# A graph network on one core: dense pass and GIN 1 in one block, weights and segments in one phase, scans in GIN 2 and GCN

## What is computed

```python
def _gin_conv(x, src, dst, wa, ba, wb, bb):
    agg = jax.ops.segment_sum(x[src], dst, num_segments=N_NODES)
    h = x + agg
    h = jnp.maximum(h @ wa + ba, 0.0)
    return h @ wb + bb
# L0: two GIN convolutions 128->64->64 and 64->256->256, then @ wl + bl
# L1 (RGCN): msg = x[src] * edge_norm; sum per (relation, dst); 4 bases mixed by w_comp
# L2 (GCN): y = x @ W.T; out = segment_sum(deg^-1/2[row] * deg^-1/2[col] * y[row], col) + bias
# L3 (GAT): 3 layers of attention with edge attributes, each with its own layer norm
x = _layernorm(x + L0(x)); x = _layernorm(x + L1(x)); x = _layernorm(x + L2(x)); x = _layernorm(x + L3(x))
```

## Time and profile before

| | us |
|---|---|
| median of 3 runs | 3941.27 (3938.68 to 3960.31) |
| the profiled execution, its own time | 3940.17 |
| its span, first to last instruction | 3938.4 |

### The profile page before, as it was taken

One profiled execution on the slowest core, in us unless ns is written; L12 is line 12 of the kernel. 1 busy time (PEld: TensorE's weight loads), 2 busy tenths in 40 slices (PEclk: granted clock), 3 DMA queues, 4 the chain that ended last, 5 costly groups with the idle time before them and its releaser, 6 DMA issues. The chain is left out here.

```text
span 3938.4 us, 83380 instructions
## 1 busy us (share of the span) xinstructions
PE 2910.5 (74%) x19323; PEld 2360.3 (60%) x19323; DVE 2669.5 (68%) x9708; ACT 2397.4 (61%) x6301; POOL 2318.7 (59%) x2526
## 2 busy tenths in 40 slices
PE   3999997815886999688588799177991778884662
PEld 2777776603443666344366699177991767883562
DVE  3999998804333566799688744387443978887873
ACT  2999987701322566466456566186771877874873
POOL 3777777776761774677578577301772027721766
PEclk7999999957997999899799999588995998876755
DMA  2667779613442444355456599265992669973541
GB/s 79 213 217 239 261 262 176 139 30 97 128 128 70 116 133 120 120 158 159 128 171 192 180 300 299 72 190 180 302 296 63 198 209 285 282 247 105 146 144 52
DMA packets 427200, 678.04 MB, mean 172 GB/s; under 512 B 81253, under 2 KB 161726, under 8 KB 427064
## 3 DMA queue, kind: packets, MB, share of 16 engines
q1 hardware_dynamic: 352664, 554.64, 44.5%
q0 software_dynamic: 74400, 121.87, 12.7%
HBM read 384.98 MB, written 295.47 MB: 173 GB/s over the span
## 5 line engine op out<-in xcount | busy, mean ns | idle before, releaser
L540 POOL DMA_INDIRECT msgs<-t_gat,row_i x600 | 577.9, 963 | 681.9 <-POOLq L123 484.9
L1636 PEld LDWEIGHTS n_p_q<-mean_col,n_sq 128*128 128x128 f32 x2352 | 309.7, 205 | 0.0
L1636 PE MATMUL n_p_q<-mean_col,n_sq 128*128 128x1 f32 x2352 | 299.4, 248 | 0.0
L2245 POOL DMA_INDIRECT out_rows<-a_res,a_stage x200 | 201.8, 1009 | 124.1 <-issue 84.5
L2263 PE MATMUL a_p_t<-ident,a_wm 128*128 128x128 f32 x600 | 120.6, 334 | 199.9 <-DVE a_wm L2344 199.8
L532 POOL DMA_INDIRECT g_ring<-t_h,g_g_stage x200 | 199.6, 998 | 77.4 <-issue 48.5
L540 POOL DMA_INDIRECT msgs<-in_x,src_i x200 | 205.6, 1028 | 64.3 <-issue 64.3
L567 POOL DMA_INDIRECT t_where<-slot_id,own_i x200 | 202.6, 1013 | 67.1 <-issue 67.1
L1475 PE MATMUL rg_p_b<-bases,rg_gt 128*128 128x512 f32 x400 | 207.0, 622 | 43.7 <-DVE rg_mg L1581 41.6
L582 POOL DMA_INDIRECT row_i<-t_where,src_i x200 | 200.8, 1004 | 64.4 <-issue 63.6
L1957 ACT ACTIVATE n_nt<-n_p_t,cxt 128x512 f32<-128x512 f32 x294 | 200.2, 681 | 61.4 <-PE n_p_t L1931 61.1
(11 more groups left out here) (391 smaller groups left out, 9335.9 us busy)
## 6 DMA issues: line engine op xcount, KB each, us to landing
n_h<-t_gat SPq DMA_DIRECT2D x294, 264.0 KB
t_gat<-n_hn SPq DMA_DIRECT2D x196, 264.0 KB
t_x<-de_x SPq DMA_DIRECT2D x196, 256.0 KB
a_h<-t_gat SPq DMA_DIRECT2D x150, 264.0 KB
t_gat<-a_hn SPq DMA_DIRECT2D x100, 264.0 KB
t_gat<-de_h SPq DMA_DIRECT2D x98, 264.0 KB
g_xd<-t_xd SPq DMA_DIRECT2D x100, 256.0 KB
n_x<-t_x SPq DMA_DIRECT2D x98, 256.0 KB
```

The lines of the kernel that those rows point to most:

```text
L540: self.nc.gpsimd.indirect_dma_start(out=self.msgs[:, c, 0:width], out_offset=None, in_=table, in_offset=bass.IndirectOffsetOnAxis(ap=idx[: ...
L1636: last = self.nc.tensor.matmul(p_q[:, j:j + 1], sq[:, j * D:(j + 1) * D], self.mean_col[:], start=True, stop=True)
L2245: nc.gpsimd.indirect_dma_start(out=self.out, out_offset=bass.IndirectOffsetOnAxis(ap=stage[:, u, j:j + 1], axis=0), in_=res[:, u, j, :], i ...
```

## The change

Six things are changed together.

1. **One start phase.** `phase_start` puts both first phases in one block. Segment loads stay on Sync, the 26 weight loads go to Scalar's queue; POOL clears, then builds the weights' constants, then tells the segment constants; Vector runs `find`, then `fold`; TensorE the two turns. `fold` also centres `bases`, `wg` and `bg` (their means over the output features are taken off).
2. **One block for the dense pass and GIN 1.** POOL runs `slot_gathers` and then at once `map_gathers`; a barrier between the two parts joins the four other engines only. Memory of the two parts is shared through `part`. TensorE waits for the message gathers and Sync for the stores of `t_xd` explicitly. `row_i` is cleared to `SLOTS + N`, a row of zeros that Sync writes into `t_h1`.
3. **GIN 1 on Vector**: the sum L1147 now stands before the scan of the same step. Added is a sum of own rows and bias `bc` that goes back to `t_xd`, 256 KB a step, so that GIN 2 needs no bias. The hidden rows are kept in `msgs` (`hidden`).
4. **GIN 2 by the scan**: four transposes of the gathered rows to two PSUM banks, a scan, a sum with `hidden`, the two layers, `p_o` with two banks. One-hot matrices, carries, the load of the own rows and the bias sum are gone; a load of the flags is added. A ring buffer is freed by its transposes.
5. **RGCN**: since inputs and weights are centred, the layer norm is a square on Scalar, a reduce on Vector, a root, a reciprocal and a scale, one step later in the pipeline; `z` and the stores too.
6. **GCN by the scan**: transposes, scan, product with `wg` into two banks, then `v` = `dis` times product plus (x2 + bg) on Vector; norm as in RGCN; the copies of the GAT rows go to Scalar.

The core of the diff:

```diff
-        net.phase_weights()
-        net.phase_segments()
-        net.phase_dense()
-        net.phase_gin1()
+        net.phase_start()
+        net.phase_dense_gin1()
...
+    def phase_start(self):
...
+            @block.sync
+            def _(sp):
+                g_load(sp)
+                w_store(sp)
+                g_store(sp, zeroes)
+            @block.scalar
+            def _(act):
+                w_load(act)
+            @block.gpsimd
+            def _(pool):
+                g_clear, g_tell = g_fill
+                g_clear(pool)
+                w_fill(pool)
+                g_tell(pool)
+            @block.vector
+            def _(dve):
+                g_find(dve)
+                w_fold(dve)
...
+    def phase_dense_gin1(self):
+        nc = self.nc
+        ctx, sb, ps, sem = self.scope("dg")
+        with ctx:
+            ring = sb("g_ring", [128, UN, G4, D])
+            block = ctx.enter_context(nc.Block())
+            self.dense_part(block, lambda n: sem("de_" + n), ring, sem)
+            nc.multi_engine_barrier([e.engine for e in (nc.sync, nc.tensor, nc.scalar, nc.vector)])
+            self.gin1_part(block, lambda n: sem("g1_" + n))
...
             def _(pool):
                 nc.gpsimd.memset(x[:].rearrange("p a b c -> p (a b c)"), 0.0).then_inc(s["cleared"], 1)
-                self.slot_gathers(pool, sb, sem)
+                self.slot_gathers(pool, ring, pool_sem)
+                self.map_gathers(pool, pool_sem)
```

GIN 1 on Vector, one step:

```diff
+                    if live(k, u, 2, AG):
+                        dve.wait_ge(s["pe_x"], i - 1)
+                        dve.wait_ge(s["dve_s"], i - 1)
+                        wait(dve, s["pe_a"], i - 3)
+                        nc.vector.tensor_tensor(rt[:, u % 2], p_x[:], at[:, u % 2], ALU.add).then_inc(s["dve_r"], 1)
                     if live(k, u, 1, AG):
...
                         nc.vector.tensor_tensor_scan(at[:, w], fl[:, v], p_t[:, w], first, ALU.mult, ALU.add).then_inc(s["dve_s"], 1)
                     if live(k, u, 2, AG):
-                        dve.wait_ge(s["pe_x"], i - 1)
-                        dve.wait_ge(s["dve_s"], i - 1)
-                        wait(dve, s["pe_a"], i - 3)
-                        nc.vector.tensor_tensor(rt[:, u % 2], p_x[:], at[:, u % 2], ALU.add).then_inc(s["dve_r"], 1)
+                        dve.wait_ge(arrived[(u - 2) % UN], 16 * (k + (0 if u < 2 else 1)))
+                        self.stored(dve, outb, k, u, 2)
+                        nc.vector.tensor_tensor(xb[:, u % 2], xd[:, (u - 2) % UN], self.each(self.bc[:]), ALU.add).then_inc(s["dve_b"], 1)
```

GIN 2 on Vector, and GCN on Vector:

```diff
+                        nc.vector.tensor_tensor_scan(at[:, w], fl[0:H, f], p_t[0:H, w], start, ALU.mult, ALU.add).then_inc(s["dve_s"], 1)
...
+                        nc.vector.tensor_tensor(rt[:, u % 2], self.hidden(i - 2), at[:, u % 2], ALU.add).then_inc(s["dve_r"], 1)
...
+                        nc.vector.tensor_tensor(x2[:, w], x2[:, w], self.each(self.bg[:]), ALU.add).then_inc(s["dve_b"], 1)
...
+                            last = nc.vector.scalar_tensor_tensor(out=v[:, w, j, :], in0=p_g[:, w % 2, j * D:(j + 1) * D],
+                                                                  scalar=self.dis[:, bass.ds((i - 3) * G4 + j, 1)],
+                                                                  in1=x2[:, w, j, :], op0=ALU.mult, op1=ALU.add)
...
+                        nc.vector.tensor_reduce(ss[:, w], sq[:, u % 2], AXX, ALU.add).then_inc(s["dve_ss"], 1)
```

More of the change, by code:

```diff
@@ L211, in nodes, with weights_parts @@
         return v[bass.ds(UN * k + u - lag, 1), :, :, :].rearrange("g p j f -> p (g j) f")
-    def phase_weights(self):
+    def weights_parts(self, sb, ps, sem):
         nc, a = self.nc, self.a
-        ctx, sb, ps, sem = self.scope("wt")
-        with ctx:
[L218 to L251, removed]
@@ new lines, in load, with store, fill @@
+        def load(act):
+            with nc.allow_non_contiguous_dma(reason="columns of biases, once"):
+                for dst, src in loads:
+                    act.dma_start(dst, src).then_inc(loaded, 16)
+        def store(sp):
+            sp.wait_ge(zeroed, 1)
+            sp.dma_start(self.t4[SLOTS:SLOTS + 128, :], spread[:, 3, :]).then_inc(stored, 16)
+            sp.wait_ge(loaded, 16 * len(loads))
+            sp.wait_ge(stored, 16)
+        def fill(pool):
+            nc.gpsimd.memset(self.ident[:], 0.0).then_inc(ready, 1)
+            nc.gpsimd.memset(ones[:], 1.0).then_inc(ready, 1)
+            nc.gpsimd.memset(self.eps[:], EPS).then_inc(ready, 1)
+            nc.gpsimd.memset(spread[:, 3, :], 0.0).then_inc(zeroed, 1)
+            nc.gpsimd.memset(begin[:], 0.0).then_inc(self.begun, 1)
+            pool.wait_ge(ready, 3)
+            nc.gpsimd.affine_select(out=self.ident[:], in_=self.ident[:], compare_op=ALU.not_equal,
+                                    fill=1.0, base=0, pattern=[[-1, 128]],
+                                    channel_multiplier=1).then_inc(ready, 1)
+            nc.gpsimd.iota(self.iota[:], pattern=[[1, 128]], base=0, channel_multiplier=0,
+                           allow_small_or_imprecise_dtypes=True).then_inc(ready, 1)
@@ L550, in slot_gathers @@
         lag = 2
+        self.msgs_got = got
+        self.rows_stored = [(stored[u], 16 * ((AG - u + UN - 1) // UN)) for u in range(UN)]
         self.resident_gather(self.src_i, a["x"], D, got, bounds_check=N - 1, oob_is_err=False)
@@ L1797, in step @@
                         nc.scalar.activation(x3t[:], p_x[:], ACT.Copy).then_inc(s["act_x"], 1)
-                    carry(4)
-                    norm((2, 3))
-                steps(act, AG, 7, step, 3)
+                    if live(k, u, 6, AG):
+                        w = (u - 6) % UN
+                        act.wait_ge(s["dve_rs"], i - 5)
+                        self.stored(act, outx, k, u, 6)
+                        wait(act, s["pe_x"], i - 6 - UN + 1)
+                        for j in range(G4):
+                            last = nc.scalar.activation(x3[:, w, j, :], v[:, w, j, :], ACT.Copy, scale=rs[:, w, j:j + 1])
+                        last.then_inc(s["act_x3"], 1)
```

933 lines of the change are left out of this document (458 added, 475 removed).

## The result

The changed kernel takes 3776.4 us (median of 4 runs, 3771.0 to 3783.8); the kernel before took 3940.0 in the same measurement. The ratio is 0.958, with a 95% interval of 0.955 to 0.961. The prediction was 3774. The profiled execution took 3777.6 us, 2.1 of it outside the span (1.8 of 3940.2 before), so stage lengths of the two traces can be set side by side.

What follows compares the result with a forecast made beforehand. No front-half stage was taken as arithmetic-bound throughout; POOL's indirect DMAs set a floor in each. Start -19, dense pass and GIN 1 -82, GIN 2 -46, RGCN -4, GCN -15 sum to -166 from 3940.2: 3774 us, range 3750 to 3825.

Steps and rivals of the forecast that it cites:

- Start: Start phase: both sets of loads in flight together, segments worked first, then weights; 43 us and 1 for the border, -19 us.
- nearly half: Start phase before the change: nearly half of its 63.1 us said to be waiting for loads that could have overlapped.
- Dense pass and GIN 1: The merged block: POOL's unbroken program ends it, with the other engines' GIN 1 hidden 57 us ahead; -82 us (-79 to -85).
- 8.5 of landing and 1 of border: Gap of 9.55 us after POOL's last scatter, read as scatters landing (8.5) and about 1 for the phase border.
- The reorder itself is worth next to nothing here: GIN 1: with the old order's 6.16 us a step the end would be S + 1101, still ahead of POOL.
- GIN 1's own terms: GIN 1 beside POOL: head 22 us, 5.2 us a step for 49 steps, tail 30 us.
- GIN 2: GIN 2 by the scan: POOL bounds it at 5.2 us a step, drain 24 us; 285 for 331, -46 us (-30 to -54).
- RGCN: RGCN: POOL keeps gathers, stage copy and z, 5.09 + 1.04 + 0.3 = 6.43 against 6.52 us; -4 us (-12 to +8).
- GCN: GCN by the scan: POOL stays the bound, 5.2 us a step, drain 26 for 33; -15 us taken (0 to -22).
- (a): Rival: POOL misses its floor; GIN 2 at 5.5 us a step (-31), GCN unchanged; 3804 us, chance 13%.
- (b): Rival: GIN 1 not hidden, scatter and added store stretch its loads to 7.2 us a step; 3815 us, chance 10%.
- (d): Rival: TensorE's clock falls in GIN 1 and 2; 4079 us, passing no change at some two thirds low-level steps; chance 2%.

Runs made afterwards that it cites:

- held runs: Changed kernel with four engines waiting for the scatters at GIN 1's head: 3834.7 us with old GIN 2 and GCN; 3877.3 with old start, sum order and RGCN.
- The table: Dense pass and GIN 1 in the changed kernel: beside the scatters 1114.2 us (old sum order 1111.0, 1111.1); held behind them 1117.8 (old order 1183.7).
- the run with PSUM operands: Changed kernel with one operand of each step's two-SBUF Vector addition moved to PSUM in GIN 2 and GCN: 3759.1 us.
- the hold: Changed kernel with Sync, TensorE, Scalar and Vector waiting at GIN 1's head for the scatters' semaphore: 5632.7 us on the chip where the kernel before took 5740.
- the early gathers: Changed kernel with POOL's first 12 message gathers issued in the start phase: 5618.1 us on the slow chip; with PSUM operands in three stages, 3737.7 on an ordinary one.

## Why the prediction was right, and where it wasn't

**Start**, -19 forecast, -20.7 measured: right by its own steps (segments from 13.55 instead of 15). The two waits for loads are 33.5 of the 63.1 us, so over half of the old phase and not "nearly half".

**Dense pass and GIN 1**, -82 forecast, -78.7 measured: the mechanism was right, POOL's sum almost to the microsecond (829.5 forecast from the stage's start to the last scatter's end, 829.3 measured; map gathers 265 and 268). Two terms were wrong and offset each other in part. The 9.55 us of the earlier trace rows were read as 8.5 of landing and 1 of border. The held runs show a landing of 1.27 us, so what filled that gap was the pause of about 8.3 at the end of a phase. In the merged block that pause didn't vanish but moved to its end, 8.4 us, for which I had a border within 4; and the landing grew to 4.5 beside GIN 1's transfers, still 4 under the 8.5 put down for it, while the map gathers took 3 more. In sum 3 over the forecast, the upper end of its bounds.

**"The reorder itself is worth next to nothing here"** was right as it stood, 0 measured. But I credited the unbroken POOL with all of the 82. The table shows that letting GIN 1 begin beside the scatters is worth 4 us with the new order and 73 with the old one. The sum was never additive, since each edit removes the excess of the same longer chain over POOL's. GIN 1's own terms were right: head 20.6 (22), step 5.16 (5.2), tail 29.8 (30).

**GIN 2**, -46 forecast, -36.5 measured (-30 to -38 in the other traces, and 0 with GIN 2 of before put back). The pace was right (the last gather issued 262.8 us after the stage's start, 261 forecast); the drain was mis-sized, 31.3 us for the 24 I took "for a shorter chain". The row of GCN, 33, that I had beside it was the nearer one.

**RGCN**, -4 forecast, -16 measured in this trace, -8 to -13 in the six others that keep its new norm. Here a step of the sum failed: 5.09 + 1.04 + 0.3 put 0.3 of issue beside the product, and the traces show four gathers, copy and product in 6.12, the product right behind the last gather. With the statistics put back 1 step of 40 is at 6.12; without them 17 to 33. POOL's rounds of 6.52 in the earlier trace rows were not its floor. How the statistics on Vector hold POOL's rounds up was not tried.

**GCN**, -15 forecast, -6 measured (-7 to -11 in the others): groups of 5.25 (5.2 forecast), but a drain of 37.6 us, last gather issued at 2057.9 to 2095.5, where I took 26 for 33. The step that failed is the shortening: the pipeline has as many steps as before, and no ordinary trace of the new GCN drains in less than 33.8 (33.1 and 36.3 in the two of the old one). One thing that lengthens it is seen: TensorE was granted 0.69 of its full clock in this drain and 0.99 in the one before, and the last group's eight matmuls take 2.13 us instead of 1.17 (timelines of TensorE before and after). Over the eight traces of the new GCN the drain (33.8 to 37.6) doesn't follow the clock (0.69 to 0.84) trace by trace, so the clock's share stays open. Both drains erred in the same direction.

```profile
2248.06 1.17 PE L1629 MATMUL gc_p_h<-wx,gc_x3t 128*128 128x132 f32 x8 [0.69 <-ACT gc_x3t L1797]
...
2089.48 2.13 PE L1682 MATMUL gc_p_h<-wx,gc_x3t 128*128 128x132 f32 x8 [0.69 <-ACT gc_x3t L1812]
```

**Vector sums beside POOL.** By the run with PSUM operands, a Vector sum of two SBUF operands held POOL's gathers and copies back by 9.5 us in GIN 2 and 8.7 in GCN, of this trace's stages (8 to 16 and 4 to 9 against the six traces). The page "SBUF — State Buffer" of the Trainium skill, section "Who interferes with whom", says that a Vector instruction with at most one SBUF input, outside its two-port modes, doesn't contend with GpSimd, and that one with two does when GpSimd reads SBUF; the traces agree, 0 of 83 and 57 of 66 stretched.

**Rivals.** (a) came nearer than its 13% said: groups at 5.27 and 5.25, not at the floor, and -42 for GIN 2 and GCN together, between its -31 and my -61. (b) didn't come: GIN 1's loads stood the scatters, 5.16 a step. (d) didn't come: GIN 2 was granted 0.93 as before. But the clock did fall in GCN, from 0.95 to 0.79 of full speed. There TensorE has room in the groups, as (d) says, but not in the drain. Redone with its own terms, (d)'s break-even lies near half of the steps at the low level, not two thirds; nothing here hangs on it.

## What to carry to other kernels

When two edits shorten the same chain beside a second engine's chain, price them in all four combinations: their sum is not their worth, and either may be free. A floor of an engine is read from rounds in which nothing else touched it, and a Vector instruction with both operands in SBUF beside POOL's transfers is worth a spare PSUM bank: two such moves brought 17 us here. Take a drain from the nearest stage that was measured, and shorten it only for a step that is seen in it. Before a border is priced at 1 us, look at every border of the trace: the 8.8 us stood at the end of RGCN before anything was changed.

## What the runs showed of the hardware

- A phase in which POOL has issued 200 or more transfers ends with 8.3 to 8.9 us in which POOL shows no instruction: 8.81 after the 200 of RGCN, 32 to 35 us behind the last of them, 8.3 to 8.5 after the 850 of dense pass and GIN 1, and 8.85 with 11 us of memsets behind their landing. After 12 transfers it was 2.9. What POOL does in it stays open.
- The last of the 4-byte scatters lands in 1.27 us in the two ordinary held runs, with nothing beside it, and in 3.8 to 6.0 beside GIN 1's loads and stores.
- On one chip the direct transfers hardly moved while POOL issued transfers (47 GB/s against 207), and the kernel before took 5740 us instead of 3940. There the changed kernel with the hold gained 2.0% (interval 1.3 to 2.7), and with the early gathers 2.4% (1.7 to 3.1); the changed kernel alone gained 4.2% on the first chip. Why that chip differs isn't known.
- RGCN runs in two paces, 6.12 and 6.59 us a step, that change within one execution: whether the one-hot build falls on a gather's beginning repeats from step to step. The stage's length varied by 8 us over the seven traces of the same RGCN with it.
